# A quarter of the shared expert's gate and up products computed during the cross-attention's last steps, and the entries of the routing table made on ScalarE

## The chip, the core and the metric

The kernel runs on one core of one Trainium2 chip. The time is that of the device in microseconds; for the kernel before it is the median of three runs. A profile is one further execution, recorded by the hardware.

Five engines work side by side, each through its own queue in order: TensorE (PE, its weight loads PEld), VectorE (DVE), ScalarE (ACT), GpSimd (POOL) and SyncE (SP), which here only issues DMAs. They wait for each other through semaphores.

## The reference

One decoder layer on 2048 tokens of width 512, in 32-bit floats: self-attention, cross-attention to a second sequence, and a mixture of experts with a shared expert. Each is added to its input.

```python
x = x + _L0_attn_ref(_layernorm(x), ...)
x = x + _L0_xattn_ref(_layernorm(x), ctx_2048, mask_BxS2_ik0, ...)   # 16 heads; its delta is normalised and scaled
x = x + _L0_ffn_ref(_layernorm(x), ...)
# _L0_ffn_ref: 64 experts, each token goes to 6 of them
scores = softmax(x @ gate_weight.T)          # the best 3 of 8 groups, then the best 6 of their experts
slot = flat * C + minimum(pos, C - 1)        # C = 192 places in each expert, pos counts its tokens in order
out = (silu(buf @ Wg.T) * (buf @ Wu.T)) @ Wd.T
y = sum over the 6 of out[slot] * topk_w
shared = silu(x @ Sg.T) * (x @ Su.T) @ Sd.T  # Sg, Su: 704 x 512, Sd: 512 x 704
return y + shared
```

## The kernel before

The tokens are 16 tiles of 128. Products in 32-bit precision are made of three passes on TensorE over halves: each operand is kept as a high half (a copy of reduced precision, made on ScalarE) and a low half (the difference, made on VectorE or GpSimd), and `matmul3` (L41 to L43) issues high with low, low with high and high with high. One program part follows the other, with a barrier between them (`end_phase`).

**Cross-attention** (`cross_phase`). Each engine has a program, written out by hand, with a loop over 16 steps t, one a tile, and after it a drain. In step t TensorE makes the scores of tile t, the output projection of tile t - 1 (`project_out`) and, for tile t - 2, the transposes of its final norm (`turn_final`) and its router's `logits`. GpSimd in the same step calculates the root for tile t - 2 (`final_rstd`), adds the residual of tile t - 1 and makes a factor for its norm (`residual`, `delta_factor`, the latter awaited by VectorE at L1532). ScalarE makes `final_norm` and `final_hi` of tile t - 2, and `route_exp`, the exponential of the router's softmax; VectorE makes `final_lo`, `output`, `delta` and the choice. SP loads inputs some steps ahead and stores results (`store_xf` the final norm, which the experts read).

Routing is done in groups of tiles, `CROSS_GROUPS`: one tile, then seven pairs, then one. For a group `group_steps` names three steps: three, four and six after its last tile. VectorE chooses the experts (`choose_experts`), TensorE counts how many earlier tokens an expert already has (`positions`), VectorE finds the places (`place_tokens`, the reduction to c_posk at L1629). Then 12 table entries for each pair, one for each token and choice, are made: a row of 192 numbers that holds the token's number at its place and zeros elsewhere (`table_entries`, L1245, on GpSimd; the last two groups, 18 entries, on VectorE at L1637, `late_entry`). `table_part` adds them up on TensorE with the one-hot rows of the experts, and VectorE enters the sum in the table (`enter_names`). The drain after step 15 holds the last three groups, which wait for each other: the count of one group needs the choice of the one before it.

**Experts** (`expert_programs`). 64 experts in 32 turns of two. While they run, the shared expert's weights and first tokens are loaded and split.

**Shared expert** (`shared_programs`), here called the tail. Four turns, each of a quad of 4 tiles (512 tokens). `hidden` makes 11 units of gate and up products, each 128 weights by 512 tokens, 12 matmuls (five pairs of a gate and an up unit, and a last one with two halves of 64); ScalarE applies silu, VectorE multiplies and the product is split. `turn_tokens` then transposes the next quad, and `down` multiplies the hidden by Sd, one tile after another, 17 matmuls each (L2752 is a tile's last). GpSimd gathers the six rows of every token from the experts' output (`gather`, L2585, two sets of buffers), VectorE adds them up with their weights (`routed`, L2663), half a tile at a time behind the hidden's chunks, and `finish` (L2673) adds the down products. The turns between the first and last are a loop on the chip.

## Time and profile before

| what | value |
|---|---|
| median of three runs | 1605.71 us (1602.22 to 1605.86) |
| the profiled execution, whole | 1597.56 us |
| its span | 1595.9 us |
| PE busy in the span | 1486.6 us (93%) |
| DVE busy | 1139.3 us (71%) |
| ACT busy | 897.5 us (56%) |
| POOL busy | 772.4 us (48%) |

A row's times are those of the profiled execution, from the start of its span. Busy time is an average over parts that have different limits, so the slices, then windows of single stages, then the timeline of a wait are read in that order. PEclk is the clock that TensorE was granted, as a share of its full speed.

### The profile page before, as it was taken

How to read it: one execution, taken by the hardware profiler on the slowest of the kernel's cores; microseconds unless marked ns; L12 is line 12 of the kernel's file. 1: busy time of each engine (PE TensorE's matmuls, PEld its weight loads, DVE VectorE, ACT ScalarE, POOL GpSimd, SP SyncE). 2: the span in 40 equal slices, each digit the busy share in tenths (PEclk: the TensorE clock that was granted, in tenths of full speed). 3: DMA queues.
4: the chain of work that ended last, by engine and by line, in shares of the span. 5: the costliest groups of instructions: out<-in, count | busy, mean ns of one | idle time of the engine just before them, and what ended most of it. 6: DMA issues, size and time to landing. Idle time of an engine off the chain costs nothing.

```text
span 1595.9 us, 30498 instructions
## 1 busy us (share of the span) xinstructions
PE 1486.6 (93%) x10360; PEld 1232.2 (77%) x10360; DVE 1139.3 (71%) x2054; ACT 897.5 (56%) x1769; POOL 772.4 (48%) x957
## 2 busy tenths in 40 slices
PE   6999998999999865499999999999999999999997
PEld 4788886778888754388888888888888888777866
DVE  5677757557888787577777777777777777565656
ACT  4565666644544331187777777777777778412111
POOL 2122234233365556265565555565555564437543
PEclk9999999999999976599999999999999999999999
DMA  6012212222211110598777787777887775437553
GB/s 205 7 55 85 62 54 91 95 71 74 75 66 41 41 54 34 202 365 294 270 266 259 275 289 264 267 267 263 277 289 263 268 262 200 137 119 225 178 177 119
DMA packets 109217, 275.48 MB, mean 173 GB/s; under 512 B 16592, under 2 KB 16592, under 8 KB 109136
## 3 DMA queue, kind: packets, MB, share of 16 engines
q1 hardware_dynamic: 91392, 223.53, 41.0%
q0 software_dynamic: 15360, 50.34, 9.8%
q8 instruction: 50, 0.82, 0.2%
q10 hardware_dynamic: 2384, 0.53, 0.2%
q14 instruction: 31, 0.25, 0.1%
HBM read 232.41 MB, written 41.94 MB: 172 GB/s over the span
## 4 chain that ended last, share of the span: by engine, by line
PE 55%; DVE 2%; DMA 1%; issue 0%; POOL 0%; ACT 0%; SPq 0%; DVEq 0%; POOLq 0%
PE e_gu L2386 18%; PE e_gu L2388 9%; PE e_dn_rest L2414 5%; PE e_tr L49 3%; PE e_dn_main L41 3%; PE e_dn_main L43 3%; PE e_dn_main L42 3%; PE h_gt L41 1%; PE h_gt L43 1%; PE h_gt L42 1%; PE h_up L43 1%; PE h_up L41 1%; PE h_up L42 1%; PE h_dn L41 1%; DVE h_acc L2663 1%; PE h_dn L42 1%
## 5 line engine op out<-in xcount | busy, mean ns | idle before, releaser
L2149 POOL TENSOR_TENSOR e_hid<-e_h_raw,e_hid 128x128 fp32r<-128x128 f32 (+1 forms) x192 | 165.6, 863 | 221.3 <-ACT e_hid L2214 221.3
L2386 PE MATMUL e_gu<-e_xT_hi_lo,e_wg 128*128 128x384 f32 (+1 forms) x768 | 231.5, 357 | 1.6 <-issue 1.6
L2386 PE MATMUL e_gu<-e_xT_hi_lo,e_wu 128*128 128x384 f32 (+1 forms) x768 | 230.4, 355 | 0.0
L2388 PE MATMUL e_gu<-e_xT_hi_lo,e_wu 128*128 128x192 f32 (+1 forms) x768 | 193.3, 252 | 0.0
L2388 PE MATMUL e_gu<-e_xT_hi_lo,e_wg 128*128 128x192 f32 (+1 forms) x768 | 193.1, 251 | 0.0
L2157 POOL TENSOR_TENSOR e_wd<-e_raw_d,e_wd 96x512 fp32r<-96x512 f32 x64 | 131.6, 2056 | 35.8 <-ACT e_wd L2199 35.8
L2386 PEld LDWEIGHTS e_gu<-e_xT_hi_lo,e_wg 128*128 128x128 f32 (+1 forms) x768 | 138.0, 180 | 6.8 <-issue 2.6
L2292 DVE TENSOR_TENSOR e_total<-e_gu,e_low 128x384 f32<-128x384 f32 (+1 forms) x192 | 105.5, 549 | 51.5 <-ACT e_low L2209 51.5
L2388 PEld LDWEIGHTS e_gu<-e_xT_hi_lo,e_wg 128*128 128x128 f32 (+1 forms) x768 | 139.8, 182 | 1.4
L2386 PEld LDWEIGHTS e_gu<-e_xT_hi_lo,e_wu 128*128 128x128 f32 (+1 forms) x768 | 137.9, 180 | 3.8
L2388 PEld LDWEIGHTS e_gu<-e_xT_hi_lo,e_wu 128*128 128x128 f32 (+1 forms) x768 | 139.7, 182 | 0.0
L2209 ACT ACTIVATE e_low<-e_gu 128x384 f32<-128x384 f32 (+1 forms) x192 | 93.0, 484 | 81.2 <-PE e_gu L2388 78.8
L2281 DVE TENSOR_TENSOR e_wg<-e_raw_g,e_wg 128x1408 fp32r<-128x1408 f32 x64 | 104.0, 1625 | 48.3 <-ACT e_wg L2190 48.3
L2585 POOL DMA_INDIRECT h_yk<-y_dram,h_idx x96 | 102.6, 1069 | 28.1 <-issue 25.9
L2137 POOL DMA_INDIRECT e_xg<-xf_dram,e_idx x96 | 96.6, 1006 | 25.3 <-issue 18.6
L2199 ACT ACTIVATE e_wd<-e_raw_d 128x1024 fp32r<-128x1024 f32 (+1 forms) x128 | 106.4, 831 | 0.9 <-DMA e_raw_d<-in_L_ffn_Wd_dram 0.9
L2298 DVE TENSOR_TENSOR e_h_raw<-e_total,e_h_raw 128x192 f32<-128x192 f32 (+1 forms) x192 | 84.7, 441 | 28.1 <-ACT e_h_raw L2204 28.1
L2281 DVE TENSOR_TENSOR e_wu<-e_raw_u,e_wu 128x1408 fp32r<-128x1408 f32 x64 | 103.9, 1624 | 0.8 <-ACT e_wu L2190 0.7
L2190 ACT ACTIVATE e_wg<-e_raw_g 128x1408 fp32r<-128x1408 f32 x64 | 87.9, 1374 | 28.4 <-DMA e_raw_g<-in_L_ffn_Wg_dram 28.4
L2624 ACT ACTIVATE h_act_g<-h_gt 128x512 f32<-128x512 f32 x20 | 12.0, 598 | 146.1 <-PE h_up L43 146.1
L505 ACT ACTIVATE s_prb<-s_prb,s_nmax 128x128 f32<-128x128 f32 x256 | 80.0, 392 | 23.2 <-DVE s_nmax L632 23.1
L2414 PE MATMUL e_dn_rest<-e_raw_d,e_h_raw 128*64 128x512 f32 (+1 forms) x384 | 89.7, 601 | 0.0
(341 smaller groups left out, 4049.3 us busy)
## 6 DMA issues: line engine op xcount, KB each, us to landing
e_raw_g<-in_L_ffn_Wg_dram SPq DMA_DIRECT2D x64, 704.0 KB, 4.3
e_raw_u<-in_L_ffn_Wu_dram SPq DMA_DIRECT2D x64, 704.0 KB, 5.7
e_raw_d<-in_L_ffn_Wd_dram SPq DMA_DIRECT2D x64, 512.0 KB, 5.9
y_dram<-e_y_main SPq DMA_DIRECT2D x64, 256.0 KB, 6.2
e_raw_d<-in_L_ffn_Wd_dram SPq DMA_DIRECT2D x64, 192.0 KB, 6.4
y_dram<-e_y_rest SPq DMA_DIRECT2D x64, 128.0 KB, 7.0
s_xr<-in_x_dram SPq DMA_DIRECT2D x16, 256.0 KB, 3.8
x_dram<-s_x SPq DMA_DIRECT2D x16, 256.0 KB, 2.5
```

The costliest lines, as they stand in the source:

```text
L41: pe.matmul(out, al, bh, start=first, stop=False)
L42: pe.matmul(out, ah, bl, start=False, stop=False)
L2137: pool.indirect_dma_start(out=xg[:, j * H:(j + 1) * H], out_offset=None, in_=xf, in_offset=bass.IndirectOffsetOnAxis(ap=idx[:, j:j + 1], a ...
L2149: pool.tensor_tensor(hid[b][1][0:n, c, :], h_raw[g.odd][b][0:n, c, 0:P], hid[b][0][0:n, c, :].bitcast(F32), ALU.subtract).then_inc(s_hl, 1)
L2157: pool.tensor_tensor(wd[b][1][0:96, 2, :], raw_d[g.odd][b][0:96, 2, :], wd[b][0][0:96, 2, :].bitcast(F32), ALU.subtract).then_inc(s_dp[b], 1)
L2199: act.activation(wd[b][0][0:rows, cs, :], raw_d[g.odd][b][0:rows, cs, :], ACT.Copy).then_inc(s_dh[b], 1)
L2281: dve.tensor_tensor(w[b][1][:], raw[b][:], w[b][0][:].bitcast(F32), ALU.subtract).then_inc(s_gul[b], 1)
L2292: dve.tensor_tensor(total[0:n, c], gu[m][0:n, :, 0:CAP], low[m][0:n], ALU.add).then_inc(s_sum, 1)
L2386: pe.matmul(bank[0:n, 0:2 * CAP], w[b][0][:, k, m:m + n], xT[:, :, k, toks], start=k == 0, stop=False)
L2388: ins = pe.matmul(bank[0:n, 0:CAP], w[b][1][:, k, m:m + n], xT[:, 0, k, toks], start=False, stop=k == KC - 1)
L2414: ins = pe.matmul(dn_rest[b * REST:(b + 1) * REST, :], h_raw[g.odd][b][0:n, c, P:CAP], raw_d[g.odd][b][0:n, c, :], start=c == 0, stop=c == 2)
L2585: pool.indirect_dma_start(out=yk[b][:, k * H:(k + 1) * H], out_offset=None, in_=y_in, in_offset=bass.IndirectOffsetOnAxis(ap=idx[b][:, k:k ...
```

## The change

The gate and up products of one quad (`AHEAD` = 2, tiles 8 to 11) leave the tail and are made in the cross-attention, as 11 `shared_unit`s of 12 matmuls:

- SP loads their weights in step 11 (five units, behind a wait for the last query projection) and step 12 (six). ScalarE copies the high halves at the end of steps 12 to 14 (`shared_hi`, 3, 4 and 4 units); GpSimd makes the low halves one step later, between `residual` and `delta_factor` (`shared_lo`).
- `final_T` keeps the transposed final norm of tiles 8 to 11 in buffers of its own.
- TensorE runs units 0 and 1 in step 14, 2 and 3 in step 15, and the other seven in the drain, between its old work. ScalarE drains each from PSUM (`shared_out`, `shared_gate` for the silus that come late), GpSimd multiplies (`shared_hidden`), and SP stores the six chunks to a DRAM buffer and waits for them ahead of the barrier.
- From step 12 on, `project_out` stands ahead of `turn_final` on TensorE, and on VectorE `final_lo` behind `output` and `row_sums` ahead of the choice.
- Table entries of tiles 0 to 14 go to ScalarE: six absolute differences of 192 columns and one clamp over 1152 columns a tile. Tile 15's six remain on VectorE (`last_entries`). What followed them in `place_tokens` is `keep_slots`.
- Buffers for all this are laid over what the self-attention alone needs.

In the tail the loop is written out. Its turns are quads 0, 1, 3 and 2; the last makes only the splitting of the hidden, loaded again from DRAM, and `down`. The next quad's transposes move into `hidden`, behind chunks 2 and 3, with a second buffer for the transposed tokens (`xT`). The running sums have four buffers, up from two, and further halves of `routed` stand behind chunks.

The diff, cut to its core:

```diff
+AHEAD = 2
...
+COPIED = 4
+FIRST_LOADS = 5
+SHARED_SPLITS = {12: range(0, 3), 13: range(3, 7), 14: range(7, 11)}
+EARLY_UNITS = {14: (0, 1), 15: (2, 3)}
...
+            def load_shared(units):
+                for i in units:
+                    parts = [(shared["w"][i % 2], i // 2 * P, 0, P)]
...
+                        sp.dma_start(f_raw[i][:, :, to:to + n], src[:, at:at + n].rearrange("(k p) m -> p k m", p=P)
+                                     ).then_inc(s_fw[i >= FIRST_LOADS], 16)
...
                 if t >= 2:
                     store_xf(t - 2)
+                if t == 11:
+                    sp.wait_ge(s_pj, filled(("q", QUADS - 1, KC - 1)))
+                    load_shared(range(0, FIRST_LOADS))
+                if t == 12:
+                    load_shared(range(FIRST_LOADS, INNER))
+            for c in range(SCN):
+                sp.wait_ge(s_fm, c + 1)
+                rows = slice(0, P) if c < FULL else slice(HALF, P)
+                sp.dma_start(shared["hidden"][c * P + rows.start:(c + 1) * P, :], f_hid[c][rows, :]).then_inc(s_fst, 16)
+            sp.wait_ge(s_fst, 16 * SCN)
...
-            def table_entries(g, i):
-                a, b = CROSS_GROUPS[g]
-                pool.wait_ge(s_posk, g + 1)
-                if g:
-                    pool.wait_ge(s_tab, g)
...
+            def shared_lo(i):
+                pool.wait_ge(s_fhi, i + 1)
+                hi, lo = shared_weight(i)
+                pool.tensor_tensor(lo, f_raw[i], hi.bitcast(F32), ALU.subtract).then_inc(s_flo, 1)
...
                     final_rstd(t - 2)
                 if t >= 1:
                     residual(t - 1)
+                for i in SHARED_SPLITS.get(t - 1, ()):
+                    shared_lo(i)
                 for m in cross_context(t):
                     context_lo(m)
                 for m in cross_fresh(t + 1):
...
-                    for i in range(CROSS_GROUPS[g][1] - CROSS_GROUPS[g][0]):
-                        if group_steps(g)[1] + i == t:
-                            table_entries(g, i)
             final_rstd(BATCH - 2)
             residual(BATCH - 1)
             delta_factor(BATCH - 1)
             final_rstd(BATCH - 1)
-            for i in range(PAIR):
-                table_entries(NG - 3, i)
+            for c in range(SCN):
+                shared_hidden(c)
...
+            def table_entries(g, i):
+                a, b = CROSS_GROUPS[g]
+                act.wait_ge(s_posk, g + 1)
+                if g == NG - 2:
+                    act.wait_ge(s_pj, len(proj_use))
+                elif g:
+                    act.wait_ge(s_tab, g)
+                rows = late_entry if g == NG - 2 else entry
+                for k in range(i * TOPK, (i + 1) * TOPK):
+                    act.activation(rows[:, k, :], iota_cap[:], ACT.Abs, bias=posk[:, k:k + 1], scale=-1.0).then_inc(s_far, 1)
+                act.wait_ge(s_far, TOPK * (a + i + 1))
+                part = rows[:, i * TOPK:(i + 1) * TOPK, :]
+                ins = act.activation(part, part, ACT.Relu, bias=token[:, a + i:a + i + 1],
+                                     scale=minus_token[:, a + i:a + i + 1])
+                if i == b - a - 1:
+                    ins.then_inc(s_entry, 1)
...
+                    for i in range(CROSS_GROUPS[g][1] - CROSS_GROUPS[g][0]):
+                        if group_steps(g)[1] + i == t:
+                            table_entries(g, i)
+                for i in EARLY_UNITS.get(t, ())[1:2]:
+                    shared_out(i)
...
                 for u in units[2:3]:
...
                         unit_out(u)
+                for i in SHARED_SPLITS.get(t, ()):
+                    shared_hi(i)
             rinv_out(BATCH - 1)
             attn_hi(BATCH - 1)
+            shared_out(4)
             final_norm(BATCH - 2)
             final_hi(BATCH - 2)
+            table_entries(NG - 3, 0)
+            shared_out(5)
+            table_entries(NG - 3, 1)
             route_exp(BATCH - 2)
             final_norm(BATCH - 1)
+            shared_out(6)
             final_hi(BATCH - 1)
             route_exp(BATCH - 1)
+            for c in range(COPIED):
+                shared_gate(c)
+            shared_out(7)
+            for i in range(PAIR):
+                table_entries(NG - 2, i)
+            for i in range(8, INNER):
+                shared_out(i)
...
-                    dve.wait_ge(s_entry, min(g, NG - 2))
+                    dve.wait_ge(s_entry, g)
                 dve.tensor_reduce(posk[:, m], counted[:, 0:n * TOPK * E].rearrange("p (a e) -> p a e", e=E), AX,
                                   ALU.add).then_inc(s_posk, 1)
+            def last_entries():
+                g = NG - 1
+                dve.wait_ge(s_posk, g + 1)
...
+                    keep_slots(g)
                 for m in fresh[0:1]:
...
+                if LAST > t >= 2:
                     final_lo(t - 2)
...
+                if t >= LAST:
+                    final_lo(t - 2)
...
+                if t >= LAST:
+                    row_sums(t)
                 for g in choosing:
                     choose_experts(g)
-                row_sums(t)
+                if t < LAST:
+                    row_sums(t)
             one, two, three = range(NG - 3, NG)
             delta(BATCH - 2)
             attn_out(BATCH - 1)
...
             rank_experts(three)
             choose_experts(three)
+            keep_slots(two)
             place_tokens(three)
+            last_entries()
+            keep_slots(three)
             enter_names(three)
             dve.wait_ge(s_tabr, NG - 2)
...
+            def shared_unit(i):
+                if i == 0:
+                    pe.wait_ge(s_er[0], exchanged(0, ("xf", QT * AHEAD + QT - 1)))
...
+                hi, lo = shared_weight(i)
+                for k in range(KC):
+                    ins = matmul3(pe, out, (hi[:, k, :], lo[:, k, :]), (fq[0][:, k, :], fq[1][:, k, :]),
+                                  k == 0, k == KC - 1)
+                ins.then_inc(done, 1)
...
+                for i in EARLY_UNITS.get(t, ())[0:1]:
+                    shared_unit(i)
...
-                if t >= 2:
+                if LAST > t >= 2:
...
                     pe.wait_ge(s_lo, len(pieces))
                 project_out(t - 1)
+                for i in EARLY_UNITS.get(t, ())[1:2]:
+                    shared_unit(i)
+                if t >= LAST:
...
                 attend_v(t)
             one, two, three = range(NG - 3, NG)
             widen(BATCH - 1)
+            shared_unit(4)
             positions(BATCH, one)
             table_part(BATCH, one - 1)
+            project_out(BATCH - 1)
             turn_final(BATCH - 2)
-            project_out(BATCH - 1)
+            shared_unit(5)
             logits(BATCH - 2)
+            shared_unit(6)
             turn_final(BATCH - 1)
             logits(BATCH - 1)
+            shared_unit(7)
             positions(BATCH, two)
+            shared_unit(8)
             table_part(BATCH, one)
+            shared_unit(9)
+            positions(BATCH, three)
+            shared_unit(10)
             table_part(BATCH, two)
-            positions(BATCH, three)
             table_part(BATCH, three)
...
+                sp.wait_ge(s_t, QT * (p + 1))
+                load_xf(sp, p + 1)
+            if p == 0:
+                for stored in free["y_stored"]:
+                    sp.wait_ge(*stored)
+                for c in range(SCN):
+                    rows = slice(0, P) if c < FULL else slice(HALF, P)
+                    sp.dma_start(raw_hid[rows, c, :], ahead_hidden[c * P + rows.start:(c + 1) * P, :]
...
+                if c:
+                    hidden_lo(p, c - 1)
+                if c in between:
+                    n, part = between[c]
+                    routed(n, range(3 * part, 3 * part + 3))
+            hidden_lo(p, FULL)
...
+        chunks(0, {3: (0, 0), 4: (0, 1)})
+        routed(1)
+        finish(0)
+        routed(2)
+        finish(1)
+        routed(3)
+        finish(2)
+        finish(3)
+        chunks(1, {1: (4, 0), 2: (4, 1), 3: (5, 0), 4: (5, 1), 5: (6, 0)})
+        routed(6, range(3, TOPK))
+        finish(4)
+        routed(7)
+        finish(5)
+        finish(6)
+        finish(7)
+        chunks(2, {0: (8, 0), 1: (8, 1), 2: (9, 0), 3: (9, 1), 4: (10, 0), 5: (10, 1)})
+        for c in range(SCN):
+            hidden_lo(3, c)
+        finish(8)
+        routed(11)
+        finish(9)
+        finish(10)
+        routed(12)
+        finish(11)
+        routed(13)
+        finish(12)
+        routed(14)
+        finish(13)
+        routed(15)
+        finish(14)
...
+                                      (xT[p % 2][0][:, k, :], xT[p % 2][1][:, k, :]), k == 0, k == KC - 1)
+                ins.then_inc(s_gu, 1)
+                if c in (2, 3) and p + 2 < turns:
+                    turn_tokens(pe, p + 1, 2 * (c - 2), 2 * (c - 1))
...
-            def turn(q, first, last):
-                hidden(q, first)
-                if not last:
-                    turn_tokens(pe, q + 1, 0, QT)
...
-                down(q, first)
```

## Rows read from the trace of the kernel before

**Rows 1.** Page, the span in 40 slices: TensorE's busy tenths and granted clock.
```profile
PE   6999998999999865499999999999999999999997
PEclk9999999999999976599999999999999999999999
```
**Rows 2.** Windows of one tail turn: PE, PEld, DVE, ACT, POOL (counts), PEclk, DMA, GB/s.
```profile
1430.48:1460.50 30.02, 30.02 (x133) 24.74 (x133) 19.93 (x31) 5.20 (x9) 24.15 (x27) 1.00 0.79 246
1460.50:1472.24 11.74, 8.04 (x35) 5.93 (x33) 6.42 (x10) 4.13 (x7) 9.16 (x11) 0.85 0.64 180
1472.24:1485.31 13.07, 13.07 (x53) 9.34 (x52) 8.79 (x14) 0.00 (x0) 2.22 (x4) 1.00 0.46 145
```
**Rows 3.** Timeline of TensorE in the tail: start, length, instruction, [idle before <- releaser].
```profile
1376.75 0.50 PE L41 MATMUL h_gt<-h_xT,h_sg 128*128 128x512 f32 x1
...
1465.35 1.35 PE L49 MATMUL h_tr<-ident,h_xf 128*128 128x128 f32 x8 [3.70 <-DVE h_xT L2649]
...
1468.21 0.63 PE L42 MATMUL h_dn<-h_sd,h_hid 128*128 128x512 f32 x1
1468.64 0.63 PE L43 MATMUL h_dn<-h_sd,h_hid 128*128 128x512 f32 x1
...
1587.54 0.49 PE L2752 MATMUL h_dn<-h_sd,h_hid_lo_over_hi 64*128 64x512 f32 x1
```
**Rows 4.** Groups by line in the tail: busy us, mean ns | idle before, releasers.
```profile
L2585 POOL DMA_INDIRECT h_yk<-y_dram,h_idx x96 | 102.6, 1069 | 28.1 <-issue 25.9 <-POOL h_idx L2579 1.1 <-DVE h_acc L2663 0.3
L2663 DVE SCALAR_TENSOR_TENSOR h_acc<-h_yk,h_w_t,h_acc 128x512 f32<-128x512 f32 x96 | 72.2, 752 | 9.3 <-DMA h_yk<-y_dram,h_idx 6.3
L2699 DVE TENSOR_TENSOR h_hid<-h_h_raw,h_hid 128x512 fp32r<-128x512 f32 x20 | 13.7, 686 | 0.1
```
**Rows 5.** Timeline of VectorE: the last output sum.
```profile
1591.70 0.69 DVE L2673 TENSOR_TENSOR h_o<-h_dn,h_acc 128x512 f32<-128x512 f32 x1
```
**Rows 6.** Windows of the cross-attention: two late steps and the drain.
```profile
556.81:576.49 19.68, 12.32 (x180) 10.21 (x172) 15.57 (x50) 5.30 (x8) 12.71 (x16) 0.83 0.12 42
591.45:610.89 19.44, 10.98 (x148) 9.04 (x140) 15.57 (x49) 5.31 (x8) 12.71 (x16) 0.79 0.13 43
610.89:654.62 43.73, 21.43 (x107) 17.29 (x107) 34.28 (x135) 4.75 (x10) 19.38 (x24) 0.58 0.07 24
```
**Rows 7.** Timeline of several engines: waits of a late step, choices, cross-attention's end.
```profile
563.80 0.81 ACT L1343 ACTIVATE a_stage<-c_x,c_fnmr,c_frstd 128x512 f32<-128x512 f32 x1 [1.56 <-POOL c_fnmr L1236]
...
564.67 1.12 PE L49 MATMUL c_ex<-ident,a_stage 128*128 128x128 f32 x4 [5.26 <-ACT a_stage L1343]
...
569.98 0.69 DVE L1524 TENSOR_TENSOR a_stage<-c_pj,c_bias_out 128x512 f32<-128x512 f32 x1 [2.77 <-PE c_pj L43]
...
639.50 0.95 DVE L1629 TENSOR_REDUCE c_posk<-a_stage 128x12 f32<-128x768 f32 x1 [2.95 <-POOL c_entry L1245]
640.55 2.96 DVE L1637 TENSOR_SCALAR a_qkT<-c_iota_cap,c_posk,c_token 128x192 f16<-128x192 f16 x12
...
654.43 0.19 DVE L1723 COPY table<-table 64x64 f32<-64x64 f32 x1
...
655.75 0.34 SPq L2061 DMA_DIRECT2D e_raw_g<-in_L_ffn_Wg_dram  x1
```
**Rows 8.** Groups by line and shape: prices of entries, halves and activations; table load.
```profile
L1245 POOL TENSOR_SCALAR c_entry<-c_iota_cap,c_posk,c_token 128x192 f16<-128x192 f16 x78 | 81.9, 1062 | 0.0
L1218 POOL TENSOR_TENSOR a_xT_lo<-a_qkT,a_xT_hi 128x512 fp32r<-128x512 f32 x8 | 10.1, 1286 | 20.9 <-ACT a_xT_hi L1323 20.9
L2204 ACT ACTIVATE e_h_raw<-e_total 128x192 f32<-128x192 f32 x128 | 45.9, 358 | 0.2 <-DVE e_total L2292 0.2
L1368 ACT ACTIVATE c_prT<-c_prT,c_not_bias,c_attend 128x1024 f32<-128x1024 f32 x32 | 39.6, 1237 | 15.1 <-DVE c_prT L1497 15.1
L491 ACT ACT_TABLE_LOAD x1 | 1.3, 1283 | 3.7 <-issue 3.7
```
**Rows 9.** DMA issues: KB each, median us from issue to landing.
```profile
e_shared_g<-in_L_ffn_Su_dram SPq DMA_DIRECT2D x1, 128.0 KB, 17.8
xf_dram<-a_stage SPq DMA_DIRECT2D x16, 256.0 KB, 2.0
```

593 lines of the change are left out of this document (345 added, 248 removed).

## The prediction

> **What bounds the kernel now.** I read the busy table in slices first. TensorE is at nine tenths or more of nearly every slice; the exceptions are the start and slices 15 to 17, the end of the cross-attention, where it falls to 6, 5 and 4 tenths and its granted clock to between 6 and 7 tenths [rows 1]. So there are two places to read. The tail (shared expert) is TensorE work from end to end; the cross-attention's last steps are a chain of short waits in which TensorE has room. The change moves a quarter of the tail's gate and up products into that room.
>
> In the tail I read one turn by its windows: 30.02 us of gate and up products in which TensorE never rests, 11.74 us in which it works 8.04 (transposes of the next quad, a wait, the first down tile), then 13.07 us of three down tiles, again without rest [rows 2]. That is 54.8 us a turn. The timeline dates the tail: first product at 1376.75, a stall of 3.70 us ahead of the last transposes of a turn, and after it matmuls 0.43 us apart; the last product ends at 1588.03 [rows 3]. The last sum ends at 1592.38 [rows 5].
>
> In the cross-attention, an ordinary late step takes 19.4 to 19.7 us with TensorE at work for 11 to 12.3, VectorE 15.6, ScalarE 5.3, GpSimd 12.7; the clock is 0.79 to 0.83. The drain after the last step takes 43.73 us with TensorE at work for 21.4, ScalarE for 4.75 and GpSimd for 19.4, but VectorE for 34.3 [rows 6]. VectorE's routing chain sets the drain; its last copy ends at 654.62, and the experts' first load is issued at 655.75 [rows 7].
>
> **The tail, part by part.** Down products of one tile take 13.07/3 = 4.36 us, so four take 17.4. With 30.0 for the products of gate and up, a turn with nothing else would be 47.4; 54.8 are there, so 7.4 go into the turn's end (transposes, the 3.70 stall, products at the slower spacing). The whole tail of before is 4 x 47.4 + 3 x 7.4 = 211.8, against 211.3 read off [rows 3].
>
> After: three times 30.0 and four times 17.4 are 159.7. The two remaining sets of transposes lie between products; at full clock I take 2.0 us for each, so 163.7. New stalls: in turns 1 and 2 the low half of the last hidden chunk (0.69) stands on VectorE behind three routed sums (0.75 us each, [rows 4]), some 2.5 us before the first down tile each time; with bank waits 1.4 and perhaps 1.5 for a slower clock behind each stall, 8 in all. TensorE would end near 1376.75 + 172 = 1549.
>
> Then the gathers bind, which before they did not: 96 of them take 1.07 us of GpSimd each with 0.29 between ([rows 4], 28.1/96), so a tile of six costs 8.2, and with the copy of its indices and that copy's wait some 8.7. Sixteen tiles are 139 us, but each pair of row buffers comes free only when VectorE has summed the tile two before. The gate and up products of the third turn end near 1376.75 + 3 x 30 + 2 x 17.4 + 4 + 4 of stalls = 1509.5; tile 10's sums, near 1515, let gather 12 start; gather 13 needs tile 11's sums, one tile's gather and a handover later, and ends its wait near 1524.6; with three tiles of 8.7 the last gather is issued near 1550.7. Some 2 us of landing, one sum of 0.75, two output sums of 0.69 [rows 5] and their handovers give a last sum at 1555 to 1559. Against 1592.4 the tail gains **33 to 37; I take 35**. Bounds: 29 (gathers at 9.4 a tile with their landing 1 us later, and the clock down at both turn ends) to 42 (no new stalls, GpSimd at its issue rate).
>
> What else moves in the tail I cost at nothing: the six loads of the stored hidden (six issues at the 0.34 us of an SP issue [rows 7]) lie ahead of output stores that are not yet due, and the copies and low halves made of them take the place of those that the fourth turn made. The weights are still split for three quads, so nothing is saved there.
>
> **The cross-attention, part by part.** Each unit is 12 products of 512 columns, 0.226 each at the pace of the tail (30.02/133, [rows 2]): 2.71 at full clock, 5.2 at half, where products are 0.43 apart [rows 3]. Eleven units are 30 or 57 us of TensorE. Steps 12 to 15 and the drain have 19.7 - 12.3, 19.4 - 11.0 and 43.7 - 21.4 free [rows 6]: room enough in the sum, but a unit queued ahead of what the chain waits for delays that chain.
>
> - *Steps 12 and 13.* Output projection ahead of the final transposes spares VectorE a wait: its output now waits 2.77 on that projection [rows 7]. Against that ScalarE gets 3 to 4 high halves, and GpSimd 3 to 4 low halves between residual and factor; the latter cost 1.29 each [rows 8], 3.9 to 5.2. The factor is awaited by VectorE, and behind it the final norm on ScalarE, which already waits 1.56 for GpSimd [rows 7]. GpSimd, though, loses the table entries, 12 x 1.06 = 12.7 per two tiles [rows 8]. I take +2 for the two steps.
> - *Step 14:* units 0 and 1 (5.5 us), one in front of the projections; TensorE's 5.26 wait for the final norm [rows 7] covers part. +4. *Step 15:* units 2 and 3, likewise, +2.5.
> - *Drain up to choice 7:* units 4 to 6 stand among projections and logits; +0.7, since VectorE is the one with the least rest.
> - *Choice 7 to choice 8:* here VectorE waits 2.95 for GpSimd's table entries and then makes twelve entries itself for 2.96 [rows 7]. Both leave its chain: **-6.2** with the semaphore step between. Price on the other engine: six ScalarE instructions of 128x192 at 0.358 and one of 128x1152 at 1.24 or a little more [rows 8], about 3.6 a tile. ScalarE has 14 us free in a step and 39 in the drain [rows 6], which covers it as long as no chain waits for the entries.
> - *Last choice to the table:* units 9 and 10 are queued ahead of the last two table parts; VectorE keeps six entries (1.5). +2.5.
> - *End:* the last halves are drained by ScalarE, multiplied by GpSimd, and stored by SP, which now waits for the landing before the barrier; a store of 256 KB lands in 2.0 [rows 9]. +2.
> - *Loads:* twelve DMAs on SP's queue at steps 11 and 12, 128 KB or 256 KB each, behind a wait for a query projection. Behind them stand the loads of x and the stores of the final norm. The nearest row, a 128 KB weight load among many, lands after 17.8 [rows 9]; two steps are 39, so I cost nothing. If they come 8 us later, the splits slip by a part of a step: +3.
>
> Sum: 2 + 4 + 2.5 + 0.7 - 6.2 + 2.5 + 2 = **+7.5**. Bounds: +2, if the units keep the clock at its upper level of 2.4 GHz through steps that now show 0.58 to 0.83 [rows 6] and speed the old work too; +18, if the units that stand directly ahead of the chain's next product (0, 2, 5 and 6) run at the lower level of 1.2 GHz, 2.5 more for each, and a part of the late entries holds VectorE.
>
> **Sum.** -35 + 7.5 = -27.5. The profiled execution took 1597.56, of which 1595.9 is span; it would become about 1570. The median of the runs shown is 1605.71, 0.5% more than the profiled one, so the median forecast is 1605.71 - 27.5 = **1578**.
>
> **Rivals.**
> (a) *Clock and queue:* the units push the DVE chain at half clock as in the upper bound: cross +18, net about -17, 1589. For it: the drain's clock of 0.58, and that the units are short and separate. Against: denser TensorE work in every row with full clock (1.00 in the turns [rows 2]).
> (b) *It doesn't do what it says:* no free TensorE time is found, the units stand on the chain with their full 30 us, less 6: about +24, net -11, 1595; with half the units at half clock (13 us more), 1608. Against: TensorE is idle for 22 of the drain's 44 us [rows 6].
> (c) *The gathers:* each tile at 9.4 instead of 8.7 and the end not hidden: tail -30, 1583. For it: in the tail nothing follows the last gather that could hide it.
> (d) *Slower, through ScalarE's function table:* absolute value and clamp now alternate with the exponential of the same steps. A table load takes 1.283 [rows 8], and two loads for each of 15 tiles are 38.5 us on the path final norm, entries, exponential of the routing. If all lie on the path, the net is +11, 1617; it decides for slower as soon as eleven of the fifteen tiles pay in full on the path. Against: of before, copy, exponential and normalisation run in one mix, and the only load ahead of the experts is the one of line 491 [rows 8].
> The Trainium skill ("ScalarE: Activation LUTs", section "Table sets: the hidden batching unit") says that cheap functions, absolute value and clamp among them, are in every set; by it, this rival does not arise. That rule speaks for the trace's single load, but no row here shows these two functions. The same page ("What ACT_TABLE_LOAD costs") adds a drain of about 1.38 us to each load of 1.283; the load agrees with the row [rows 8], and with the drain thirty switches would be 80 us and the time an estimated 1658.
>
> **How the numbers follow.** Forecast 0.58, with its own range 1565 to 1590; (a) 0.17; (b) 0.08, two thirds of it still faster; (c) 0.08; (d) 0.06; the rest, 0.03, is a wait that I have not seen, on the slower side. About 0.3% (4.8 us) is what a measurement of this kernel can tell from no change. Faster by more: 0.58 + 0.17 + 0.08 + 0.04 = 0.87; within 0.05 (the dear side of (b) and part of (d)); slower 0.08. Range: -42 + 2 = -40 gives 1566, lowered by 2 for a median that differs from the profile's; -29 + 18 = -11 gives 1595, raised by 3 for (b). So 1564 to 1598.
>
> **What would show it.** In the slices, TensorE above 7 tenths and a higher clock in slices 14 to 16. Steps 14 and 15 longer by 2 to 4 us each, the wait for GpSimd's entries gone from the position reduction, the gap from VectorE's last copy to the experts' first load longer than 1.1 us by the store. One or two table loads in ScalarE's first 660 us, not thirty. In the tail three stretches of 30 us, transposes at full clock, TensorE ending near 1549 and the last gathers after it. The forecast is wrong if the cross-attention ends after 673, or if the tail lasts longer than 187 us from its first product to the last sum.

## The result, and the profile after

The changed kernel takes 1591.64 us (median of four runs, 1587.95 to 1592.59) against 1604.84 for the kernel before: a ratio of 0.9924, interval 0.9904 to 0.9944. It is faster by 13.2 us, less than half of the forecast 27.7. The profiled executions, 1587.95 and 1597.56 whole, lie 9.6 apart, their spans 9.7; so the rows below account for 9.7, and some 3.5 us of the difference of the medians stand in no row.

The same dates read from the profile after answer to [rows 3, 5, 7]. The fence has rows of the timeline of several engines: start, length, engine, line, instruction.

```profile
543.52 0.75 DVE L1683 SCALAR_TENSOR_TENSOR c_x<-a_stage,c_fac,a_qkT 128x512 f32<-128x512 f32 x1
...
674.37 0.19 DVE L1888 COPY table<-table 64x64 f32<-64x64 f32 x1
...
677.47 0.34 SPq L2258 DMA_DIRECT2D e_raw_g<-in_L_ffn_Wg_dram  x1
...
1396.56 0.50 PE L41 MATMUL h_gt<-h_xT,h_sg 128*128 128x512 f32 x1
...
1581.40 1.29 DVE L2884 TENSOR_TENSOR h_o<-h_dn,h_acc 128x512 f32<-128x512 f32 x2
```

The first row is the residual's addition for tile 10, in step 12; in the kernel before it starts at 542.12. I use the stretch from it to the end of the last copy into the table as the measure for the cross-attention, since it holds the new order, the units and the late entries, and nothing of the jitter ahead of it: 112.50 us before (654.62 - 542.12), 131.04 after. The whole difference of the spans is then:

| stretch | before | after | difference |
|---|---|---|---|
| start to tile 10's addition | 542.12 | 543.52 | +1.4 |
| that to the table's end | 112.50 | 131.04 | +18.5 |
| table's end to the experts' first load | 1.13 | 2.91 | +1.8 |
| experts | 721.00 | 719.09 | -1.9 |
| tail, first product to the last sum | 215.64 | 186.13 | -29.5 |

The first and fourth line I don't put down to the change: over the runs below tile 10's addition starts between 540.5 and 546.1, and the experts take 718.3 to 722.3. The forecast had -35 for the tail and +7.5 for the cross-attention with its store. Both came out worse, by 5.5 and by 12.8. Of the two signs that the forecast named for being wrong, one came: the cross-attention ends at 674.56, after 673; the tail, 186.13, stays under 187.

The cross-attention after, step by step (one addition to the next, tiles 10 to 15): 20.05, 20.00, 19.19, 24.28, 12.85, against 15.38, 19.67, 14.97, 19.44, 11.98. So step 12 is 4.7 us longer, although no unit runs in it; steps 14 and 15, with two units each, are longer by 4.2 and 4.8. TensorE's busy tenths rose in slices 14 to 17 and its granted clock in slices 15 to 17, as expected; slice 18 fell, since the cross-attention now reaches into it (compare [rows 1]):

```profile
PE   6999998989999977869999999999999999999997
...
PEclk9999999999999988879999999999999999999998
```

### The profile page after: what moved, and what is told of

Same layout as the page of the kernel before. It is cut to its first block, busy times and chain, and to the rows that moved or that the text cites. A ratio compares the mean times of both kernels' runs of the same rounds, so it can differ in the third digit from the quotient of the medians.

```text
span 1586.2 us, 30306 instructions
## 1 busy us (share of the span) xinstructions
PE 1489.7 (94%) x10344; PEld 1230.7 (78%) x10344; DVE 1134.6 (72%) x2032; ACT 956.1 (60%) x1891; POOL 711.0 (45%) x885
## 4 chain that ended last, share of the span: by engine, by line
PE 47%; POOL 3%; DMA 2%; issue 2%; DVE 1%; ACT 1%; another core or an unknown queue 1%; SPq 0%; POOLq 0%; DVEq 0%
PE e_gu L2583 19%; PE e_gu L2585 9%; PE e_dn_rest L2611 5%; PE e_tr L49 3%; PE e_dn_main L41 3%; PE e_dn_main L43 3%; PE e_dn_main L42 3%; POOL h_yk L2792 2%; DMA h_yk<-y_dram,h_idx 1%; DVE h_acc L2875 1%; DMA h_xf<-xf_dram 1%; DMA e_xg<-xf_dram,e_idx 1%; PE h_gt L41 0%; PE h_up L43 0%
## 5 line engine op out<-in xcount | busy, mean ns | idle before, releaser
L2583 PEld LDWEIGHTS e_gu<-e_xT_hi_lo,e_wg 128*128 128x128 f32 (+1 forms) x768 | 138.4, 180 | 5.8 <-issue 1.6
L2387 ACT ACTIVATE e_wg<-e_raw_g 128x1408 fp32r<-128x1408 f32 x64 | 88.3, 1379 | 13.2 <-DMA e_raw_g<-in_L_ffn_Wg_dram 13.2
L2387 ACT ACTIVATE e_wu<-e_raw_u 128x1408 fp32r<-128x1408 f32 x64 | 88.3, 1380 | 0.3 <-DMA e_raw_u<-in_L_ffn_Wu_dram 0.3
```

What stands on the lines that cost most here:

```text
L2387: act.activation(w[b][0][:], raw[b][:], ACT.Copy).then_inc(s_guh[b], 1)
L2583: pe.matmul(bank[0:n, 0:2 * CAP], w[b][0][:, k, m:m + n], xT[:, :, k, toks], start=k == 0, stop=False)
```

## Experiments on the cross-attention

The measure is always the stretch from tile 10's addition to the table's end, 112.50 before and 131.04 after. One code agrees with itself to some 2 us: the changed cross-attention gave 128.96 in the run `c1_tail` below, and that of `b1_unit7` lies between 110.09 and 111.09 in five executions (`b1`, `f0`, `f1`, `g0`, `g1`). The other kernels of this part were profiled once each.

**What of the 18.5 are units?** Four kernels, each a part undone.

`a1_no_units`: the dictionaries that place units and splits are empty, and the calls of the drain, the loads and the store are deleted.

```diff
-SHARED_SPLITS = {12: range(0, 3), 13: range(3, 7), 14: range(7, 11)}
-EARLY_UNITS = {14: (0, 1), 15: (2, 3)}
+SHARED_SPLITS = {}
+EARLY_UNITS = {}
...
-            shared_unit(7)
```

> Leaves out the eleven shared units of the cross-attention with all that belongs to them (weight loads, halves, products, draining, store); the new order of steps 12 to 15 and the table entries on ScalarE stay, and so does the tail, which loads other rows of the same size in place of the stored hidden, so the shared part of tiles 8 to 11 is not the reference's. Measure: from the start of the residual's addition for tile 10 to the end of the last copy into the table, 112.5 us before and 131.0 after the change. Theory (the growth of 18.5 is queueing on TensorE: units ahead of what the routing chain waits for, and the projection put ahead of the final transposes): about 10 of it are the units, the new order alone keeps some 6 to 8, the entries give back 6: 112 to 115. Rival 1 (all of it is the units and their helpers, the order is free): 106 to 107. Rival 2 (entries on ScalarE cost the chain more than they give): over 118.

Measured: 121.57. Without a single unit the stretch is still 9 us longer than before. The number lies in the range of rival 2 (entries on ScalarE cost more than they give); the next run shows that its cause is another.

`a2_no_units_old_order`: the same and

```diff
-        LAST = BATCH - XQ
+        LAST = BATCH
...
-            project_out(BATCH - 1)
             turn_final(BATCH - 2)
+            project_out(BATCH - 1)
```

> As the one before, without the units and all that belongs to them (the shared part of tiles 8 to 11 is not the reference's), and in addition the order of steps 12 to 15 and of the drain's projection is that of the kernel before. What is left of the change in the cross-attention is the move of the table entries to ScalarE. Same measure (112.5 before, 131.0 after). Theory: the forecast's own term, minus 6.2 between the last two choices, holds when nothing else stands on the chain: 106 to 107. Rival (ScalarE's entries take the place of GpSimd's on the chain): 111 to 113.

Measured: 103.94, below the expectation. The move of the entries alone is worth 8.6 us, 6.6 of them between choice 7 and choice 8 (16.14 to 9.50, from the start of one choice to the start of the next; the forecast's term was 6.2). So rival 2 is out. And the new order alone, `a1` less `a2`, costs 17.6: it was dearer than I thought.

`a3_units_old_order`: the edit of `LAST` and of the drain's projection on the changed kernel, with all units.

> The changed kernel with all its units; only the order of steps 12 to 15 (final transposes ahead of the projection on TensorE, low half ahead of the output and choice ahead of the row sums on VectorE) and of the drain's projection is put back to that of the kernel before. Same measure (112.5 before, 131.0 after). Theory: the new order itself costs 4.7 in step 12, where no unit runs yet, and a unit plus a projection in front of the transposes of steps 14 and 15 costs about 3 more: 122 to 125. Rival (the order was what kept the units off the chain, so undoing it costs): 131 to 135.

Measured: 113.05, far below. With units the order costs 131.04 - 113.05 = 18.0, the same as without; and eleven units with all their helpers cost 113.05 - 103.94 = 9.1. One execution took 1567.01 against 1596.46 for one of the kernel before on the same chip.

`a4_thin_units`: one product in place of twelve.

```diff
-                for k in range(KC):
-                    ins = matmul3(pe, out, (hi[:, k, :], lo[:, k, :]), (fq[0][:, k, :], fq[1][:, k, :]),
-                                  k == 0, k == KC - 1)
+                ins = pe.matmul(out, hi[:, 0, :], fq[0][:, 0, :], start=True, stop=True)
```

> The changed kernel, each shared unit of the cross-attention made of one product in place of twelve (so the shared part of tiles 8 to 11 is not the reference's); loads, halves, draining, multiplication, store and every wait stay. Same measure (112.5 before, 131.0 after). Theory (TensorE's queue): nearly the whole cost of the units is TensorE's time ahead of the chain, so about 10 to 12 fall away: 119 to 121. Rival (the helpers: halves on GpSimd between residual and factor, halves and draining on ScalarE, the store): 128 to 131, hardly less than with whole units.

Measured: 120.53, as the theory has it and within 1.1 us of no units at all (121.57). So without TensorE's full products the units cost nothing in sum. That each helper is free does not follow: from tile 15's addition to the table's end `a4` takes 30.64 and `a1` 27.11, and steps 13 and 15 are shorter in `a4` by 3.7 and 2.2, which makes up for it. Why they are shorter the runs don't show; what makes the end longer is shown under "Units at the chain".

**Why the order costs 18.** Step 12 of the changed kernel (timeline of TensorE, then of VectorE; brackets: idle before, and releaser):

```profile
550.20 0.80 PE L41 MATMUL c_pj<-c_wo_hi,c_aT_lo 128*128 128x512 f32 x1
...
554.92 0.60 PE L49 MATMUL c_ex<-ident,a_stage 128*128 128x128 f32 x4
557.48 0.27 PE L41 MATMUL c_ex<-c_gate_hi,a_shared_x_lo 128*128 128x64 f32 x1 [1.96 <-DVE a_shared_x_lo L1692]
...
560.00 1.94 PE L1954 MATMUL c_ex<-c_prT,c_pick 128*32 128x128 f32 x32
...
555.12 0.69 DVE L1671 TENSOR_TENSOR a_stage<-c_pj,c_bias_out 128x512 f32<-128x512 f32 x1 [2.69 <-PE c_pj L43]
...
560.11 0.22 DVE L1697 TENSOR_REDUCE c_lneg<-c_ex 128x1 f32<-128x64 f32 x1 [2.52 <-PE c_ex L43]
562.01 0.96 DVE L1652 RECIPROCAL c_rinv<-c_ex 128x128 f32<-128x128 f32 x1 [1.67 <-PE c_ex L1954]
```

The same step of `a3_units_old_order`, which starts 2.54 us earlier (540.98):

```profile
547.66 1.12 PE L49 MATMUL c_ex<-ident,a_stage 128*128 128x128 f32 x4
548.42 0.78 PE L41 MATMUL c_pj<-c_wo_hi,c_aT_lo 128*128 128x512 f32 x1
...
552.67 0.19 PE L41 MATMUL c_ex<-c_gate_hi,a_shared_x_lo 128*128 128x64 f32 x1
...
554.03 1.08 PE L1954 MATMUL c_ex<-c_prT,c_pick 128*32 128x128 f32 x32
...
552.88 0.69 DVE L1671 TENSOR_TENSOR a_stage<-c_pj,c_bias_out 128x512 f32<-128x512 f32 x1 [2.39 <-PE c_pj L43]
...
554.67 0.21 DVE L1697 TENSOR_REDUCE c_lneg<-c_ex 128x1 f32<-128x64 f32 x1
```

The final norm's way is transposes (TensorE), high half (ScalarE), low half (VectorE), logits (TensorE). In the old order the transposes stand ahead of the projection, so the two halves are made while TensorE projects, and the logits follow the last projection without a gap. In the new order the transposes come at the projection's end; TensorE rests 1.96 us for the halves, and after that rest it runs at or near its lower level of 1.2 GHz (granted clock 0.53 over the logits and 0.50 over the row sums; 1.00 over both in `a3`): most of the logits' products are spaced 0.21 and not 0.11, all twelve take 2.59 and not 1.43, the row sums 1.94 and not 1.08. VectorE, which waited for nothing at its maximum of the logits in the old order, waits 2.52 there and another 1.67 for the row sums. In return the projection begins only 0.76 us sooner in the step (6.68 against 7.44 after the addition), and more slowly (4.72 for twelve products, granted clock 0.57, against 4.25 at 0.64); VectorE's wait for it is 2.69, where `a3` has 2.39.

The same wait for the logits stands in each of the other three steps:

```profile
576.93 0.23 DVE L1697 TENSOR_REDUCE c_lneg<-c_ex 128x1 f32<-128x64 f32 x1 [1.68 <-PE c_ex L43]
...
600.16 0.23 DVE L1697 TENSOR_REDUCE c_lneg<-c_ex 128x1 f32<-128x64 f32 x1 [1.42 <-PE c_ex L43]
...
619.54 0.23 DVE L1697 TENSOR_REDUCE c_lneg<-c_ex 128x1 f32<-128x64 f32 x1 [1.82 <-PE c_ex L43]
```

With 2.52 in step 12, the waits for the row sums (1.67, 0.81, 0.82, 1.67) and two for the high half in steps 14 and 15 (1.66 and 1.87) they come to 15.9 us; the four steps are 15.7 longer than in `a3`, where the waits at logits and row sums come to 1.6. The rest of the 18.0, 2.3, lies behind tile 14's addition. In step 13 the logits keep the upper pace, 0.11, so the trip costs without the slower clock too.

`d1_pe_order` puts back TensorE's half of the order alone (the condition in front of `turn_final`, and the drain's projection):

```diff
-                if LAST > t >= 2:
+                if t >= 2:
                     turn_final(t - 2)
...
-                if t >= LAST:
-                    turn_final(t - 2)
```

> The changed kernel with TensorE's order alone put back (final transposes ahead of the projection in steps 12 to 15 and in the drain); VectorE keeps the new order. Same measure (131.0 after the change, 113.05 with both put back). Theory (the transposes behind the projection put the trip through ScalarE and VectorE, and TensorE's rest in it, on the chain): TensorE's order is nearly all of the 18: 113 to 117. Rival (VectorE's low half behind the output, and row sums ahead of the choice, are the cause): 126 to 131.

`d2_dve_order` puts back VectorE's, with the same edit at `final_lo`, and `row_sums` behind the choice:

> The changed kernel with VectorE's order alone put back (low half ahead of the output, choice ahead of the row sums); TensorE keeps the projection ahead of the final transposes. Same measure (131.0 and 113.05). Theory (TensorE's order): 128 to 135, since the low half now also holds the output while it waits for the transposes behind the projection. Rival (VectorE's order): 114 to 118.

Measured: 124.27 and 126.11. Both theories fell, and so did the rivals: TensorE's order alone gives back 6.8, VectorE's 4.9, both together 18.0. The logits' row in step 12 shows why one is not enough, first in `d1_pe_order`:

```profile
557.48 0.27 PE L41 MATMUL c_ex<-c_gate_hi,a_shared_x_lo 128*128 128x64 f32 x1 [2.40 <-DVE a_shared_x_lo L1692]
```

and in `d2_dve_order`:

```profile
557.26 0.27 PE L41 MATMUL c_ex<-c_gate_hi,a_shared_x_lo 128*128 128x64 f32 x1 [1.50 <-DVE a_shared_x_lo L1692]
```

In the first, VectorE's low half stands behind the output, which waits for the projection; in the second, the output stands behind the low half, which waits for transposes that come after the projection. Either way the low half is made after the projection, with TensorE at rest. How much of the 18 is the row sums' place ahead of the choice was not tried by itself.

**Units at the chain.** Choice 7 to choice 8 is 15.19 us after the change, hardly less than the 16.14 before, although entries alone brought it to 9.50. VectorE's row after the choice, with TensorE's queue ahead of it:

```profile
651.34 0.77 PE L41 MATMUL c_sc<-a_shared_x_hi,a_shared_up_lo 128*128 128x512 f32 x1
...
656.71 0.30 PE L2031 MATMUL c_sc<-c_diag_pos,c_chosen 128*64 128x128 bf16 x2
...
657.33 0.42 DVE L1763 TENSOR_REDUCE c_lmax<-c_sc 64x2 f32<-64x256 f32 x1 [4.67 <-PE c_sc L2036]
```

Unit 7 is issued ahead of the positions. It runs for 5.4 us at a granted clock of 0.51, and the choice, done at 652.5, waits for it. `b1_unit7` is `a3` with two lines exchanged:

```diff
-            shared_unit(7)
             positions(BATCH, two)
+            shared_unit(7)
```

> The kernel with all units and the old order of steps 12 to 15 (from tile 10's addition to the table's end 113.05 us, from choice 7 to choice 8 14.02); one edit more: unit 7 is issued on TensorE behind the positions of the last pair, no longer ahead of them. Theory: VectorE's 4.18 us wait for those positions is unit 7 alone, which ran there at the lower clock; it falls to under 1 and choice 7 to choice 8 to about 10, the whole to 109. Rival (units 7 to 9 now all stand between the positions and the last tables, so the end gives it back): 112 to 114.

Measured: 111.09, between theory and rival (110.09 to 110.69 in the four later executions of that cross-attention). The wait for the positions fell from 4.18 to 0.82 and the products of positions from 2.12 to 1.02, 4.5 together, but choice 7 to choice 8 fell by 2.4 alone (14.02 to 11.58) and the end gave back 0.4. What took the difference is on VectorE: GpSimd's multiplications of the hidden, which in `a3` lay beside the products of positions, lie in `b1` beside three small instructions of the choice, and these grew from 0.58 to 2.67 in all. The dearest of them, in `a3`, then in `b1` with the multiplications:

```profile
642.64 0.18 DVE L1718 TENSOR_TENSOR c_gone<-c_iota,c_gidf 128x24 f32<-128x24 f32 x1
...
642.55 1.23 DVE L1718 TENSOR_TENSOR c_gone<-c_iota,c_gidf 128x24 f32<-128x24 f32 x1
...
639.93 5.06 POOL L1320 TENSOR_TENSOR a_qkT<-a_qkT 128x512 f32<-128x512 f32 x4 [10.64 <-ACT a_qkT L1514]
```

The same is seen behind choice 8. VectorE's last six entries take 1.53 without units (`a2_no_units_old_order`):

```profile
643.35 1.53 DVE L1764 TENSOR_SCALAR a_qkT<-c_iota_cap,c_posk,c_token 128x192 f16<-128x192 f16 x6
```

and 3.42 in `a3_units_old_order`, where GpSimd multiplies two chunks of the hidden in the same stretch:

```profile
649.08 3.42 DVE L1784 TENSOR_SCALAR a_qkT<-c_iota_cap,c_posk,c_token 128x192 f16<-128x192 f16 x6
...
649.43 1.34 POOL L1320 TENSOR_TENSOR a_qkT<-a_qkT 128x512 f32<-128x512 f32 x1 [7.95 <-ACT a_qkT L1505]
650.91 1.28 POOL L1320 TENSOR_TENSOR a_x<-a_x 64x512 f32<-64x512 f32 x1
```

`a4_thin_units`, with the same two multiplications and a twelfth of the units' products, has 3.30, so it is not TensorE's work. The products of positions (`a_stage<-a_stage,c_posn`, two) went from 1.02 to 2.12 beside the other four multiplications; in `a4`, where these begin only as the products end, they take 1.02. So of the 9.1 that the units cost in the old order, 3.4 are the wait for unit 7 and 3.0 (1.1 + 1.9) VectorE's instructions beside GpSimd. The Trainium skill ("SBUF — State Buffer", section "SBUF: two separate sides") says that VectorE and GpSimd share one pair of ports under an exclusive lock, which would be this; the runs show the stretching beside GpSimd, and that it is gone where the multiplications are not beside it, not the lock.

## Experiments on the tail

After the change the tail's windows answer to [rows 2]: the first turn's products with the next quad's transposes, its four down tiles, the third turn's products, the last eight down tiles.

```profile
1396.56:1428.76 32.20, 32.15 (x150) 26.48 (x149) 15.85 (x25) 9.08 (x17) 12.81 (x14) 1.00 0.65 216
1428.76:1451.07 22.31, 19.22 (x70) 13.38 (x68) 17.71 (x28) 1.86 (x3) 16.19 (x17) 0.92 0.65 193
1504.75:1534.82 30.07, 30.07 (x134) 24.89 (x133) 16.07 (x26) 5.19 (x9) 14.04 (x17) 1.00 0.52 176
1534.82:1579.86 45.04, 39.57 (x137) 27.65 (x135) 35.61 (x55) 5.19 (x9) 33.15 (x32) 0.89 0.74 227
```

The products are as forecast (30.07; 32.20 with transposes); four down tiles are 22.31 where 17.4 and a stall of 2.5 were forecast. Two rests of TensorE and one of GpSimd stand out in the timeline:

```profile
1445.24 0.79 PE L41 MATMUL h_dn<-h_sd,h_hid 128*128 128x512 f32 x1 [2.55 <-DVE h_o L2884]
...
1490.62 0.50 PE L2990 MATMUL h_dn<-h_sd,h_hid_lo_over_hi 128*128 128x512 f32 x1 [2.20 <-DVE h_hid_lo_over_hi L2894]
...
1540.47 0.71 POOL L2789 COPY h_idx<-slot 128x6 uint32<-128x6 uint32 x1 [0.82 <-DVE h_acc L2875]
```

The second was in the sum, as 2.5; for waits like the first the sum had 1.4 in the whole tail: in the first turn the second tile's output sum stands behind six routed sums of the third, and TensorE needs its bank. Gather 12 starts at 1540.47, 143.9 after the first product; the forecast had 1515 - 1376.75 = 138.

`c1_tail` takes these rests away:

```diff
         finish(0)
+        finish(1)
         routed(2)
-        finish(1)
-        routed(3)
         finish(2)
+        routed(3)
         finish(3)
-        chunks(1, {1: (4, 0), 2: (4, 1), 3: (5, 0), 4: (5, 1), 5: (6, 0)})
-        routed(6, range(3, TOPK))
+        chunks(1, {1: (4, 0), 2: (4, 1), 3: (5, 0), 4: (5, 1)})
+        routed(6)
...
-        chunks(2, {0: (8, 0), 1: (8, 1), 2: (9, 0), 3: (9, 1), 4: (10, 0), 5: (10, 1)})
+        chunks(2, {0: (8, 0), 1: (8, 1), 2: (9, 0), 3: (9, 1), 4: (10, 0)})
+        routed(10, range(3, TOPK))
```

> The changed kernel; edits in the tail's VectorE program alone: in the first turn the second tile's output sum ahead of the routed sums of the third tile (and the third's ahead of the fourth's), and in the second and third turn the half of routed sums that stood behind the last hidden chunk now behind its low half. Tail from its first product to the last sum: 186.1 after the change, 180 forecast. Theory (the 6 us missing are TensorE waiting 3.0 for that output sum and 2.2 and 2.0 for that low half, with slower products behind): 179 to 182. Rival (the gathers set the end whatever TensorE does): 185 to 187.

Measured: tail 184.53, 1.6 less; the theory fell. Nor is the 1.6 a gain that is shown: the changed tail took 185.3 to 188.5 in five more executions (`a3`, `b1`, `d1`, `d2`, `f0`). The first turn's down tiles did shrink to 18.2, but new rests came: 2.71 us for the third quad's tokens (a transfer that SP issues behind output stores) and 2.22 for another output sum. The third turn began at 107.7 after the first product, where it had been 108.2, and gather 12 at 144.2, where it had been 143.9.

The other way is to let the gathers go earlier. `f1_all` does so in two turns, beside the moved output sums and an earlier load of the third quad's tokens, and takes `b1`'s cross-attention; `f0_order_unit7` is `b1` itself, timed.

```diff
-        chunks(1, {1: (4, 0), 2: (4, 1), 3: (5, 0), 4: (5, 1), 5: (6, 0)})
+        routed(4)
+        chunks(1, {1: (5, 0), 2: (5, 1), 3: (6, 0), 4: (6, 1)})
...
-        chunks(2, {0: (8, 0), 1: (8, 1), 2: (9, 0), 3: (9, 1), 4: (10, 0), 5: (10, 1)})
+        routed(8)
+        chunks(2, {0: (9, 0), 1: (9, 1), 2: (10, 0), 3: (10, 1), 4: (11, 0)})
+        routed(11, range(3, TOPK))
```

> The same kernel as b1_unit7 (old order of steps 12 to 15 and of the drain, unit 7 behind the positions of the last pair, all units in place), now timed. Theory (the new order was the step that ate the gain; with it undone the sum of the forecast, about 28 to 30 us less than before, holds): ratio to before 0.980 to 0.983. Rival (the single looks flattered it): 0.988 or more.

> As f0_order_unit7, and in the tail the gathers' chain is let go earlier: VectorE adds tile 4 ahead of the second turn's chunks and tile 8 ahead of the third's (in stretches where it rested), tiles 5, 6 and 9 to 11 move up accordingly, output sums of tiles 1, 2, 13 and 14 go ahead of the next tile's routed sums, and SP loads the third quad's tokens ahead of the output stores. Theory (the tail's end follows the start of the gather for tile 12, 143.9 us after the first product, which waits for tile 10's sums): that gather starts before 136, the tail is 176 to 180 in place of 186, and the ratio to before 0.975 to 0.979. Rival (gathers run at the pace of the memory, or TensorE's own rests hold the end): tail 183 to 186.

Measured: `f0_order_unit7` 1571.78 us against 1604.65, ratio 0.9806, interval 0.9769 to 0.9844, as the theory has it. `f1_all` 1566.72, ratio 0.9766, interval 0.9739 to 0.9793. Its profile, however, taken on the longest of its six executions, has a tail of 187.98, with gather 12 at 142.4 after the first product. TensorE rests there in the second turn, with no releaser in its row; VectorE's product of the first chunk's gate and up ends as the rest does:

```profile
1442.61 0.50 PE L41 MATMUL h_gt<-h_xT,h_sg 128*128 128x512 f32 x1 [3.69 <-issue]
...
1441.86 1.29 DVE L2907 TENSOR_TENSOR h_h_raw<-h_up,h_act_g 128x512 f32<-128x512 f32 x2
```

To tell that rest from the edit: `g0_all_again` is `f1_all`; `g1_tail8` has the early sums in the third turn and the end alone.

> The same kernel as f1_all, a second look: its first profile showed TensorE at rest for 3.7, 0.6 and 1.0 us in the second turn with no releaser shown, while six tiles were gathered without a pause. If those rests belong to the kernel (gathers let go early keep TensorE from something), they are there again and the tail is 186 to 189; if they were that one execution's, the tail is 178 to 182.

> As f0_order_unit7 (tail 185 to 188 in its looks, gather for tile 10 at 123 to 125 us after the first product), and in the tail only the third turn and the end changed: VectorE adds tile 8 ahead of that turn's chunks, where it rested 6.9 us, tiles 9 to 11 move up by as much, and output sums of tiles 9, 13 and 14 go ahead. The first two turns are as in the changed kernel. Theory (the tail's end hangs on a chain of gathers that starts with tile 10's and waits for routed sums): that gather starts at 115 to 117, the one for tile 12 at 136 to 139 in place of 144 to 145, tail 178 to 181. Rival (TensorE, or the pace of the gathers, holds the end): 184 to 188.

Measured: `g0_all_again` 1559.03 in its one execution, tail 179.77, gather 12 at 134.3 after the first product (last row of the fence), as the theory of `f1_all` has it. But the rest is there again, ahead of the same product, 65.9 after the tail's first and 66.1 in `f1_all`, and here its row names VectorE's product:

```profile
1437.67 1.29 DVE L2907 TENSOR_TENSOR h_h_raw<-h_up,h_act_g 128x512 f32<-128x512 f32 x2
...
1438.42 0.80 PE L41 MATMUL h_gt<-h_xT,h_sg 128*128 128x512 f32 x1 [3.99 <-DVE h_h_raw L2907]
...
1506.80 0.19 POOL L2790 COPY h_idx<-slot 128x6 uint32<-128x6 uint32 x1 [2.77 <-DVE h_acc L2876]
```

So this rest is the edit's. Tile 4's sums now stand ahead of the second turn's chunks on VectorE and wait for their gathers; VectorE multiplies the first chunk behind them, and TensorE needs that chunk's banks for its third. The 8.2 us between the two executions are something else: over the second turn and its down tiles (1427.45 to 1492.51 and 1422.95 to 1480.42) the difference is 7.6, of which 5.2 are TensorE's products at a lower granted clock (0.92 and 0.85, against 0.96 and 1.00) and 2.4 rests. Why the clock differed stays open.

`g1_tail8` took 1564.48, ratio 0.9765, interval 0.9726 to 0.9805; in its profile the tail is 188.44, gather 10 at 122.1 and gather 12 at 142.7, all outside the theory. It rests for 3.75 us too in the second turn, whose code is that of the changed kernel, but for another reason: the first chunk's products end at 1438.44, and ScalarE begins its silu only at 1446.42. VectorE's product and then TensorE follow.

```profile
1446.42 0.60 ACT L2836 ACTIVATE h_act_g<-h_gt 128x512 f32<-128x512 f32 x1 [32.72 <-remote]
...
1447.05 0.69 DVE L2906 TENSOR_TENSOR h_h_raw<-h_up,h_act_g 128x512 f32<-128x512 f32 x1 [10.77 <-issue]
...
1447.79 0.80 PE L41 MATMUL h_gt<-h_xT,h_sg 128*128 128x512 f32 x1 [3.75 <-issue]
```

What held ScalarE for 8 us the row does not name ("remote" is another core or a queue that the profile does not know); it stays open.

Counted from the third turn's first product, the profiles fall into two groups: to the last sum it is 77.9 us in the changed kernel and 78.5 in `f0_order_unit7` (76.4 to 77.6 in `a3`, `b1`, `d1` and `d2`); with the sums moved up it is 72.0 in `f1_all`, 71.9 in `g0_all_again` and 72.1 in `g1_tail8`. So moving that turn's sums up is worth 4 to 6 us behind its start. That it works by letting the gathers go earlier is argued, since the edits move output sums too; for it speaks that the last sum comes 13.3 to 14.5 us after the last gather's copy of indices in all these profiles. When the third turn begins varied between executions by as much as the gain: 107.9 and 116.0 after the first product for the same code. The timed ratios of `f0`, `f1` and `g1` overlap, so the tail edits' gain is shown by that stretch alone, not by the times.

## Why the prediction was right or wrong

The median, 1591.64, lies within 1564 to 1598, but outside the forecast's own 1565 to 1590, and the gain is under half of what was forecast. Two readings of the rows were off: the clock of slices 15 to 17 is 7, 6 and 5 tenths [rows 1], not between 6 and 7, and the steps of 19.4 and 19.7 us were taken for ordinary where every second one takes 15.0 to 15.4. No priced term of the sum rests on either, but the room in the short steps (TensorE at work for 12.0 and 11.4 in them) was never read.

- **The step that failed is the order of steps 12 and 13.** The forecast said that the projection ahead of the final transposes "spares VectorE a wait", set the halves against that, and put steps 12 and 13 at +2. They took +5.0, and over steps 12 to 15 and the drain the order costs 18.0 (`after` less `a3`) with units and 17.6 (`a1` less `a2`) without. Nor does the order spare the wait: without units VectorE waits for the four projections 1.49, 3.15, 1.78 and 3.15 in the new order (`a1`) and 1.29, 2.66, 1.91 and 2.89 in the old (`a2`). With units it is 2.69 (new) and 2.39 (old) in step 12 and in neither order shows in steps 13 to 15. The rows of step 13, `a1` and then `a2`:

```profile
574.44 0.69 DVE L1651 TENSOR_TENSOR a_stage<-c_pj,c_bias_out 128x512 f32<-128x512 f32 x1 [3.15 <-PE c_pj L43]
...
568.91 0.69 DVE L1651 TENSOR_TENSOR a_stage<-c_pj,c_bias_out 128x512 f32<-128x512 f32 x1 [2.66 <-PE c_pj L43]
```

I had priced what the new order lets start earlier and not what it sends to the back: the halves between transposes and logits, which the old order hid behind the projection.
- **The units' sum was right by luck**: 4 + 2.5 + 0.7 + 2.5 = 9.7 forecast, 9.1 measured (`a3` less `a2`), but in other places. Steps 14 and 15, put at 6.5, cost 0.8; from tile 14's addition to the table's end, put at 3.2, it is 8.2, of which 4.5 lie between choice 7 and choice 8, where the forecast had no cost for them. GpSimd's multiplications, which it took for hidden, are 3.0 of that by way of VectorE.
- **The entries were right, and then lost**: -6.2 forecast, -6.6 between the choices by themselves (-8.6 in the whole stretch), -0.9 in the changed kernel, since unit 7 and the multiplications on GpSimd stand in the place of the wait. Their price on ScalarE was 3.6 a tile; six at 0.36 (2.17) and the clamp at 1.35 make 3.5:

```profile
L1474 ACT ACTIVATE c_entry<-c_iota_cap,c_posk 128x192 f16<-128x192 f16 x78 | 28.2, 445 | 0.0
L1477 ACT ACTIVATE c_entry<-c_entry,c_token,c_minus_token 128x1152 f16<-128x1152 f16 x13 | 17.5, 1347 | 0.4
L491 ACT ACT_TABLE_LOAD x1 | 1.3, 1283 | 3.5 <-issue 3.5
L1514 ACT ACT_TABLE_LOAD x1 | 1.3, 1283 | 0.0
```

- **Rival (d) is out**: two table loads in the changed kernel, one ahead of ScalarE's first copy (L491, as in [rows 8]) and one at the first silu, where thirty were feared. The Trainium skill's rule on sets ("ScalarE: Activation LUTs", "Table sets: the hidden batching unit") agrees with these rows.
- **Rival (a)**, units on the chain at the lower clock, gave +18 for the cross-attention and 1589, nearest to both, by the wrong way: unit 7 did run so (5.4 us), but taking it off the chain is worth 2.0 to 3.0 (113.05 in `a3`, 110.09 to 111.09 behind that edit), and with all units in the old order the stretch is 0.55 longer than before. The granted clock of the stretch rose from 0.71 to 0.84, and to 0.91 in `a3`.
- **Rival (b)**, the units' full 30 us on the chain, is out by the 9.1. **Rival (c)**, gathers at 9.4 a tile, gave -30 for the tail, which is the measured number, but mostly by another way. Gathers 12 to 15 do follow each other at 9.4 (28.3 for three, where the forecast's dates make 27.0), which is 1.3 of the 5.5; gather 12 itself starts 6 us late. GpSimd's own pace is that of before, 1.08 a gather with 0.30 between (1.07 and 0.29 in [rows 4]):

```profile
L2792 POOL DMA_INDIRECT h_yk<-y_dram,h_idx x96 | 103.6, 1079 | 28.7 <-issue 24.6 <-POOL h_idx L2789 4.1
```

- **The store** was right in this profile: the gap to the experts' first load grew by 1.8, forecast 2. Over the other kernels with the store the gap is 1.2 to 2.7, and 1.2 in the two without it.
- **The tail** is a mis-sized term: -29.5 against -35, at the bound named for it, though mostly not by that bound's cause. From the third turn's last product to the last sum 47.7 us were measured (1534.98 to 1582.69) and 47.5 forecast. But that product ends 138.4 after the first, not 132.8: the stalls up to there, put at 4 us with the slower products behind them, came to 9.5. Of these 5.8 are rests of TensorE, the wait for an output sum behind routed sums among them, and 3.7 products that took longer than in the sum. Taking rests away (`c1`) did not bring this back.

With the order undone the time comes out near the forecast, but by luck: the cross-attention with its store is 1.25 us longer than before (`a3`: 113.05 and a gap of 1.83) where +7.5 was forecast, and the tail 29.8 shorter (185.88) where it was 35, so two wrong terms nearly cancel. `f0_order_unit7` is 32.9 us below the kernel before by the medians (25 to 37 by its interval).
